# Attention scores of a macaron transformer kernel: one fp32 product replaced by three fp32r products of high and low parts

## The reference, cut to what matters

```
scale = DH ** (-0.5)                                   # H = 16 heads, DH = 64, 512 tokens
q = jnp.einsum('btc,hdc->bhtd', x, Wq)
k = jnp.einsum('btc,hdc->bhtd', x, Wk)
...
v = jnp.einsum('bthe,bted->bhtd', mix_v, proj_v)       # top-2 of 8 experts per head
scores = jnp.einsum('bhid,bhjd->bhij', q * scale, k)
probs = jax.nn.softmax(scores, axis=-1)
attn = jnp.einsum('bhij,bhjd->bihd', probs, v)
...                                                    # top-2 of 8 output experts, Wo
```

## Time and profile before

| | |
|---|---|
| median of three runs | 2796.3 us (2793.99 to 2802.63) |
| the profiled execution's own time | 2803.4 us |
| its span, first to last instruction | 2801.5 us |
| mean granted clock of TensorE | 0.966 of 2.4 GHz |
| PE busy | 2579.3 us, 92% of the span |
| DVE busy | 2187.3 us, 78% |
| ACT busy | 1855.6 us, 66% |
| POOL busy | 737.2 us, 26% |

### The profile page before, as it was taken

How to read it: one execution, slowest core, us unless ns; L and a number is a source line. 1 busy time by engine, 2 the same in 40 slices (tenths; PEclk the granted TensorE clock), 3 DMA queues, 4 the chain that set the end, 5 groups by cost and what they waited for, 6 DMA issues and landing times.

```text
span 2801.5 us, 51283 instructions
## 1 busy us (share of the span) xinstructions
PE 2579.3 (92%) x17437; PEld 1712.1 (61%) x17437; DVE 2187.3 (78%) x3233; ACT 1855.6 (66%) x4430; POOL 737.2 (26%) x564
## 2 busy tenths in 40 slices
PE   4499999998999998999899999999999999899997
PEld 2366665665666655666565665656566665666665
DVE  5688776889889788987987889797777878775552
ACT  2256665867678576875776867687677768666563
POOL 1000000345045214512540443064144315410000
PEclk8699999999999999999999999999999999999998
DMA  3234353564565646546464654666466465545434
GB/s 134 71 114 119 97 145 97 140 174 125 144 155 146 165 112 170 152 125 163 132 171 109 171 146 138 147 167 173 112 176 172 130 159 144 161 124 149 108 80 91
DMA packets 753407, 385.77 MB, mean 138 GB/s; under 512 B 421568, under 2 KB 678656, under 8 KB 752768
## 3 DMA queue, kind: packets, MB, share of 16 engines
q1 hardware_dynamic: 749216, 380.79, 51.4%
q10 hardware_dynamic: 3936, 1.70, 0.2%
HBM read 274.91 MB, written 115.87 MB: 139 GB/s over the span
## 4 chain that ended last, share of the span: by engine, by line
PE 59%; DVE 22%; issue 9%; ACT 3%; DMA 3%; POOL 2%; SPq 1%; DVEq 0%; ACTq 0%; POOLq 0%
PE ps L723 12%; PE ps L732 11%; PE ps L745 11%; PE ps L792 7%; DVE h_ring L1223 6%; PE ps L712 6%; PE ps L798 3%; DVE h_nmax L1043 3%; PE ps L805 2%; DVE h_ring L1233 2%; PE ps L764 1%; POOL h_ring L659 1%; PE ps L832 1%; ACT h_prob L891 1%; DVE h_wide_a L1195 1%
## 5 line engine op out<-in xcount | busy, mean ns | idle before, releaser
L891 ACT ACTIVATE h_prob<-ps,h_nmax 128x512 f32<-128x512 f32 x1024 | 710.6, 696 | 141.6 <-DVE h_nmax L1043 139.6
L1043 DVE TENSOR_REDUCE h_nmax<-ps 128x2 f32<-128x1024 f32 x512 | 621.9, 1215 | 142.7 <-PE ps L723 142.4
L732 PE MATMUL ps<-ident,h_prob 128*128 128x128 f32 x4096 | 623.6, 279 | 27.0 <-DVE h_probT L1283 15.2
L732 PEld LDWEIGHTS ps<-ident,h_prob 128*128 128x128 f32 x4096 | 481.2, 144 | 197.8 <-issue 120.9
L723 PE MATMUL ps<-h_qk 64*128 64x512 f32 x2048 | 587.6, 651 | 0.9 <-ACT h_prob L891 0.8
L668 POOL TENSOR_TENSOR h_wide_c<-h_wide_c,h_ring 128x512 f32<-128x512 f32 x240 | 331.1, 1380 | 731.7 <-DVE h_ring L1233 731.7
L1011 ACT ACTIVATE h_probT<-ps 128x512 f32<-128x512 f32 x796 | 478.7, 601 | 60.8 <-PE ps L732 57.9
L745 PE MATMUL ps<-h_probT,h_v_sb 128*64 128x256 f32 x4096 | 502.7, 388 | 5.8 <-DMA h_v_sb<-v_d 3.6
L745 PEld LDWEIGHTS ps<-h_probT,h_v_sb 128*64 128x64 f32 x4096 | 273.4, 137 | 314.5 <-issue 145.2
L1223 DVE TENSOR_TENSOR_SCAN h_ring<-h_ring 128x512 f32<-128x512 f32 x256 | 397.3, 1552 | 37.6 <-POOL h_ring L659 21.3
L659 POOL TENSOR_TENSOR h_ring<-h_m_xpad,h_m_b_rows 128x512 f32<-128x512 f32 x256 | 349.7, 1376 | 259.0 <-DVE h_m_xpad L1342 250.0
(11 more groups left out here) (222 smaller groups left out, 2678.5 us busy)
## 6 DMA issues: line engine op xcount, KB each, us to landing
h_mix_diag<-mix_blocks SPq DMA_DIRECT2D x128, 512.0 KB, 3.9
v_d<-h_v_mixed SPq DMA_DIRECT2D x128, 256.0 KB, 4.3
h_v_sb<-v_d SPq DMA_DIRECT2D x128, 256.0 KB, 3.4
at_d<-h_att SPq DMA_DIRECT2D x128, 256.0 KB, 2.8
h_mo_diag<-mo_blocks SPq DMA_DIRECT2D x128, 256.0 KB, 3.4
h_att<-at_d SPq DMA_DIRECT2D x128, 256.0 KB, 3.7
h_m_b_rows<-dbl_d SPq DMA_DIRECT2D x128, 256.0 KB, 4.3
h_m_c_rows<-dbl_d SPq DMA_DIRECT2D x128, 256.0 KB, 4.3
```

The lines of the kernel that those rows point to most:

```text
L732: ins = pe.transpose(ps[:, TB + v % 2, k * P:(k + 1) * P], prob[:, v % NB, k * P:(k + 1) * P], ident[:, :])
L891: act.activation(prob[:, v % NB, :], ps[:, SB + v % 4, :], ACT.Exp, bias=nmax[:, p, j, o:o + 1], accum_out=den[:, p, j, o:o + 1]).then_inc ...
L1043: dve.tensor_reduce(nmax[:, p, j, :], ps[:, SB + 2 * w % 4:SB + 2 * w % 4 + 2, :], X, ALU.max, negate=True).then_inc(sem("row_max"), 1)
```

## The change

q and k are now kept as a high part in fp32r (`qk_hi`) and a low part in fp32r (`qk_lo`), and the scores are the sum of three products, as in `three_passes`. ACT reads the PSUM bank twice: once to `qk_hi`, once to the fp32 tile `qk_raw` (one buffer). POOL computes `qk_lo` = `qk_raw` - `qk_hi`. `pq` moves from step 8p-5 to 8p-9 and `pk` from 8p-4 to 8p-5; `drive` moves one step earlier. To make room in SBUF, `x_prep`, `x_post`, `nrm` and `nT` become one tile `x_io`, `g_rest` is written over `gates`, `chosen` holds one gate's choice at a time, and the weights' staging tile at the start lies in `prob` and not in `qk`.

```diff
-            + [(8 * p - 5, "pq", p) for p in range(PAIRS)] + [(8 * p - 4, "pk", p) for p in range(PAIRS)],
+            + [(8 * p - 9, "pq", p) for p in range(PAIRS)] + [(8 * p - 5, "pk", p) for p in range(PAIRS)],
...
-            x_prep = t("x_prep", [P, J, D])
-            x_post = t("x_post", [P, J, D])
-            nT = t("nT", [P, S])
+            x_io = t("x_io", [P, J, D])
+            ln["nrm"] = nrm = x_io
+            nT = x_io[:, :, :].rearrange("p j c -> p (j c)")
...
-            g_rest = t("g_rest", [P, J, H * E])
-            chosen = t("chosen", [P, 2, J, H * E])
+            chosen = t("chosen", [P, J, H * E])
...
-            qk = t("qk", [P, 2, 2, S])
+            qk_hi = t("qk_hi", [P, 2, 2, S], F32R)
+            qk_lo = t("qk_lo", [P, 2, 2, S], F32R)
+            qk_raw = t("qk_raw", [P, S])
...
@@ SyncE, post: the second load of x
-                                if u == 14:
+                                if u == 20:
                                     if n >= 1:
                                         sp.wait_ge(sem("x_out"), 16 * n)
-                                    sp.dma_start(x_post[:, :, :], rows(x_in[n])).then_inc(sem("x_post_in"), 16)
+                                    if n + 2 < NJ:
+                                        wait_full(sp, "gate", 1, n + 2)
+                                        sp.wait_ge(sem("nT_split"), n + 3)
+                                    sp.dma_start(x_io[:, :, :], rows(x_in[n])).then_inc(sem("x_post_in"), 16)
...
@@ SyncE, prep: the first load of x
-                                    if n >= 2:
-                                        sp.wait_ge(sem("normed"), n)
-                                    sp.dma_start(x_prep[:, :, :], rows(x_in[n])).then_inc(sem("x_prep_in"), 16)
+                                    if n >= 3:
+                                        sp.wait_ge(sem("x_out"), 16 * (n - 2))
+                                    else:
+                                        wait_full(sp, "gate", 1, n - 1)
+                                        sp.wait_ge(sem("nT_split"), n)
+                                    sp.dma_start(x_io[:, :, :], rows(x_in[n])).then_inc(sem("x_prep_in"), 16)
...
@@ GpSimd
+                    def low_part(what, p, n):
+
+                        m = 0 if what == "pq" else 1
+                        wait_taken(pool, what, p, n)
+                        pool.tensor_tensor(qk_lo[:, p % 2, m, :], qk_raw[:, :],
+                                           qk_hi[:, p % 2, m, :].bitcast(F32), ALU.subtract).then_inc(sem("qk_lo"), 1)
...
-                                    if u == SCAN_AT[v] - 1:
+                                    if u == SCAN_AT[v] - 2:
                                         drive(n, v)
...
+                            elif kind == "heads":
+                                for p in range(PAIRS):
+                                    for what in ("pq", "pk"):
+                                        if u == AT[what, p] + 2:
+                                            low_part(what, p, n)
...
@@ TensorE, scores
                         if j == 0:
-                            wait_taken(pe, "pk", p, i)
+                            pe.wait_ge(sem("qk_lo"), 2 * (PAIRS * i + p + 1))
                         if w >= 2:
                             pe.wait_ge(sem("prob"), 2 * w - 2)
-                        for o in range(2):
-                            ins = pe.matmul(ps[:, SB + 2 * w % 4 + o, :], qk[o * DH:(o + 1) * DH, p % 2, 0, j * P:(j + 1) * P],
-                                            qk[o * DH:(o + 1) * DH, p % 2, 1, :], start=True, stop=True)
+                        for k_, (q_, k) in enumerate(((qk_hi, qk_hi), (qk_lo, qk_hi), (qk_hi, qk_lo))):
+                            for o in range(2):
+                                ins = pe.matmul(ps[:, SB + 2 * w % 4 + o, :],
+                                                q_[o * DH:(o + 1) * DH, p % 2, 0, j * P:(j + 1) * P],
+                                                k[o * DH:(o + 1) * DH, p % 2, 1, :], start=(k_ == 0), stop=(k_ == 2))
...
@@ ScalarE, take of pq and pk
-                            ins = act.activation(qk[:, c % 2, 0 if what == "pq" else 1, :], bank, ACT.Copy)
+                            act.activation(qk_hi[:, c % 2, 0 if what == "pq" else 1, :], bank, ACT.Copy)
+                            if PAIRS * n + c >= 1 or what == "pk":
+                                act.wait_ge(sem("qk_lo"), 2 * (PAIRS * n + c) + (what == "pk"))
+                            ins = act.activation(qk_raw[:, :], bank, ACT.Copy)
                         elif what == "norm":
-                            if n >= 1:
-                                wait_full(act, "gate", 1, n - 1)
-                                act.wait_ge(sem("nT_split"), n)
-                            ins = act.activation(nT[:, :], bank, ACT.Copy)
+                            ins = act.activation(nT, bank, ACT.Copy)
...
@@ VectorE, top2: chosen is free once the other gate's choice is stored; the rest is written over gates
-                            if a == 1 and i >= 1:
+                            if a == 0 and i >= 1:
                                 dve.wait_ge(sem("mo_out"), 16 * i)
                             link(dve.tensor_copy(pick, key))
...
-                                out=g_rest[:, :, :].rearrange("p j c -> p (j c)"),
+                                out=gates[:, a, :, :].rearrange("p j c -> p (j c)"),
```

More of the change, by code:

```diff
@@ L107, in macaron_kernel @@
         ln = {"stats": sb("stats", [P, J, 6]), "mv": sb("mv", [P, J, 2]), "var_e": sb("var_e", [P, J]),
-              "rstd": sb("rstd", [P, J]), "nrm": sb("nrm", [P, J, D])}
-        nrm = ln["nrm"]
+              "rstd": sb("rstd", [P, J])}
         def links(eng, name):
@@ L278, in macaron_kernel @@
         for kind, n in BASE:
-            for u in range(-8, 110):
+            for u in range(-10, 110):
                 live_at.setdefault(step_of(kind, n, u), []).append((kind, n, u))
@@ L412, in macaron_kernel @@
                 w_load[name] = w.rearrange("h d c -> (h d) c").rearrange("(a p) c -> p a c", p=P)
-            qk_f32 = qk[:, :, :, :].rearrange("p a b s -> p a (b s)").rearrange("p a (n c) -> p a n c", c=P)
+            qk_f32 = prob[:, :, :].rearrange("p (a b) s -> p a (b s)", a=2).rearrange("p a (n c) -> p a n c", c=P)
             att_flat = att[:, :, :, :].rearrange("p a j c -> p (a j c)")
@@ L578, in _ @@
                                         att2_load(n, c)
-                                if u == 14:
+                                if u == 20:
                                     if n >= 1:
                                         sp.wait_ge(sem("x_out"), 16 * n)
-                                    sp.dma_start(x_post[:, :, :], rows(x_in[n])).then_inc(sem("x_post_in"), 16)
+                                    if n + 2 < NJ:
+                                        wait_full(sp, "gate", 1, n + 2)
+                                        sp.wait_ge(sem("nT_split"), n + 3)
+                                    sp.dma_start(x_io[:, :, :], rows(x_in[n])).then_inc(sem("x_post_in"), 16)
                                 if u == AT["out", 0] + 3:
                                     wait_taken(sp, "out", 0, n)
-                                    sp.dma_start(rows(x_res[b] if kind_ == 0 else out[b]), x_post[:, :, :]
+                                    sp.dma_start(rows(x_res[b] if kind_ == 0 else out[b]), x_io[:, :, :]
                                                  ).then_inc(sem("x_out"), 16)
@@ L639, in _ @@
                                     sp.wait_ge(sem("chosen"), 2 * n + 2)
-                                    sp.dma_start(rows(mo_d[n]), chosen[:, 1, :, :]).then_inc(sem("mo_out"), 16)
+                                    sp.dma_start(rows(mo_d[n]), chosen[:, :, :]).then_inc(sem("mo_out"), 16)
                                 for c in range(NCV):
@@ L1081, in take @@
                             dve.wait_ge(sem("x_post_in"), 16 * (n + 1))
-                            x_ = x_post[:, :, :].rearrange("p j c -> p (j c)")
+                            x_ = x_io[:, :, :].rearrange("p j c -> p (j c)")
                             ins = dve.scalar_tensor_tensor(out=x_, in0=bank, scalar=0.5, in1=x_, op0=ALU.mult,
@@ L1094, in top2 @@
                         JH = J * H
-                        g = (gates[:, a] if r == 0 else g_rest)[:, :, :].rearrange("p j (h e) -> p (j h) e", e=E)
+                        g = gates[:, a, :, :].rearrange("p j (h e) -> p (j h) e", e=E)
                         top = g_top[:, :].rearrange("p (n a) -> p n a", a=1).broadcast_to([P, JH, E])
@@ L1098, in top2 @@
                         key = g_key[:, :, :]
-                        pick = chosen[:, a, :, :].rearrange("p j (h e) -> p (j h) e", e=E)
+                        pick = chosen[:, :, :].rearrange("p j (h e) -> p (j h) e", e=E)
                         linked()
@@ L1132, in mix_gates @@
```

(8 more changed lines are left out.)

## The result

The changed kernel took 2834.48 us (median of four, 2833.36 to 2839.47) against 2797.23 us before. The ratio is 1.0135, with an interval of 1.0114 to 1.0155: some 38 us slower. The forecast was 2721 us.

What follows compares the result with a forecast made beforehand. PE was taken as the limit without the scan, DVE with it. Savings of 53 us without and 31 us with the scan, less 10 for contention, gave 74, rounded 75, from 2796.3: 2721 us; range 2663 to 2825 us (0.80).

Steps and rivals of the forecast that it cites:

- What bounds the kernel: Whole schedule: PE is the limit without the scan; with the scan DVE is full and PE is not.
- the stretches: Eight pair periods beside the scan, each granted part of PE's 1.04 us: 0.44 each, 31 us; periods without scan 53 us.
- The halves of the array: PE's scores: fp32r halves work side by side, three slots in 0.80 us, saving 0.26 us a time, 133 us.
- B: Rival on PE's scores: fp32r does not split the array, 220 us more work, 2986 to 3016 us; chance 0.13.
- E: Rival on PE's scores: each slot waits for its weight load, up to 118 us more, 2914 us; chance 0.03.
- ACT's copies and wait, the bank, the shared tiles and their loads: ACT, PSUM and loads: 154 us more copying, bank held 0.6 us longer, later loads; all taken as 0 us.
- POOL's time: POOL: 256 subtractions at 1.38 us add 353 us, from 26% to some 39% of the span.
- DVE against POOL: DVE slowed by POOL: 0.18 us per subtraction, 47 us in all, 25 beside the scan, 10 on the path.
- C: Rival: POOL and DVE in each other's way, 0.77 us per subtraction beside the scan, 108 us, 2851 us; chance 0.07.
- The rule on weight loads that I weighed: PE's scores: a weight load overlaps matmuls in flight only when its row group differs; weighed as the ground for E.

Runs made afterwards that it cites:

- run 1: The changed kernel with each of POOL's 256 subtractions cut to 8 of 512 columns, all waits, copies and matmuls kept; 2764 us, ratio 0.9876.
- run 7: The changed kernel with three fp32r products only for the 52 pairs without a scan, low parts by POOL, the other pairs fp32; 2791 us, ratio 0.9960.
- run 11: Run 1 with the high times high product alone, the other two products of the scores left out; 2702 us, ratio 0.9633.
- run 8: Run 1 with ACT's second copy cut to 8 columns too; 2762 us, ratio 0.9856.
- run 2: The changed kernel with ACT's fp32 copy written where the low part will stand, POOL subtracting in place, so ACT doesn't wait; 2832 us, ratio 1.0110.
- run 14: Run 7 with ACT's fp32 copy going where the low part will stand, so that ACT waits for nobody; 2790 us, ratio 0.9945.
- run 3: The kernel before with the shared tiles and SyncE's changed waits alone, fp32 scores and steps as before; 2802 us, ratio 1.0000.
- run 5: The changed kernel with low parts made by DVE from PSUM, without POOL's subtractions and ACT's second copy; 2922 us, ratio 1.0416.

## Why the prediction was wrong, point by point

- **What bounds the kernel.** Right with the scan, where DVE is full; too simple without it. By the stretches I let 84 us of 133 come out, 63%; without the subtractions (run 1) 38 of 87 did, 44%. By period it was 22 us with the scan, where I had 31, and 22 without it, where I had 53. PE was busy all through the 14 us that I read, but as its work gets shorter it waits more for DVE and ACT (run 7) and its clock falls (run 11). I had no term for either.
- **The halves of the array.** Right in kind (B and E fell: matmuls start in twos, and the second slot's loads start 0.1 us after the scores do, while the first two matmuls run), wrong in size. I took 0.80 us from a full-height group and measured 0.89. What was missing is the 0.09 us at the far end, where the matmuls go back from two halves to full height; it stood in the second 0.53 us of the fp32 scores. That is 46 us of PE.
- **ACT's copies and wait, the bank, the shared tiles and their loads.** Right at zero, as far as tried: runs 8, 2, 14 and 3. Run 8 leaves a short copy of 8 columns, so it prices the copy's length and not its being there.
- **POOL's time.** Near: 1.43 us for each subtraction against 1.38, but `drive` itself went from 1376 to 1576 ns (1409 in run 1, with `drive` as early), which I left out. 416 us more, not 353.
- **DVE against POOL.** This is the step that failed. I took 0.13 us of DVE for each us of POOL, 47 us in all, 25 of them beside the scan and 10 of those on the path. Run 1 against the changed kernel shows 108 us of DVE and 70 of path; beside the scan it is 95 us of DVE and 63 of path. Two errors. I read the price from the scan alone, and the scan's own part came out below it (31 us); the read and all the other operations of DVE, which I left out, took the larger share. And I put 40% of DVE's extra time beside the scan on the path, where 66% came out (63 / 95). A reason for that would be that POOL, which waits for DVE's read, hands DVE's delay back to it; no run separates this from DVE's being full in more of the time than I counted.
- **TensorE's clock.** No term of mine. It was 0.953 to 0.955 in the changed kernel's executions and 0.957 to 0.965 in run 1's. The executions of the kernel before differ with it: those at 0.958 to 0.960 took 2812 us in the middle and those at 0.966 to 0.968 took 2797, so some 2 us for each 0.001 (an estimate from these; the means of the two kernels are 0.954 and 0.960). By that, some 12 of the 70 us came by way of the clock. It is no cause beside the subtractions, since they alone differ between the two kernels; that TensorE's longer waits are what lowered it is my reading and was not tested.
- **The rivals.** The result is C's mechanism. That the time is near its 2851 us is in part luck: C has 53 us of saving and 108 of cost, where 38 and 70 were measured. Cut by period, run 1 and the changed kernel differ by 63 us in the 73 periods with the scan and by 7 in the others: 63 / 146 = 0.43 us for each subtraction beside the scan, above the 0.38 from which C decides. I gave it 0.07, and against it stood only the mean excess of 0.18 us. The row that spoke for it, DVE at 98%, was the one that counted.
- **The sum with what was measured.** 38 us of saving less 70 of cost is 32 us slower, against the forecast's 84 - 10 = 74 faster. Of these 106 us, 60 are the subtractions and 46 PE's saving: 29 for its size (63% of 46) and 17 for how much of it comes out. The 32 are no check of the 38 and 70, which are both differences to run 1; the changed kernel beside its own kernel before was 37 us slower.

## What to carry to other kernels

A second engine that looks idle is not free room if its operations hold up those of the engine that is the limit: price the work by a run with idle copies of it, not by its own busy time, and put them where the real ones will stand (here they stood elsewhere and cost 95 us in place of 70). Where two limits alternate along a schedule, apply a trade between them only in the stretches where the first one binds: the change loses 1.35% applied everywhere and gains 0.4 to 0.55% applied to the 52 pairs without a scan. A busy time that rises with an unchanged count of instructions is the first thing to look for in the profile after.

## What the runs showed of the hardware

- fp32r matmuls of 64 rows on the two halves of the array run side by side, 0.23 us for two of 512 columns at full clock (2.4 GHz), and weight loads hide under them. Going back from the halves to full height costs 0.09 us, for fp32r and for fp32. The first slot of a group is about 0.1 us longer too, but with full-height matmuls just as with the halves (0.32 and 0.33 us). The Trainium skill (TensorEngine Tiling, Key Properties) says that a change of the tiling mode drains TensorE; the 0.09 us on the way back agree with it, and on the way in no extra time shows. The rule on weight loads that I weighed (in the Trainium skill, TensorE: Matmul & The Clock Gate, it stands under The mechanism) does not hold here: the loads of the second slot start at 1404.40 us, in the same rows in which the first two matmuls run from 1404.30 on, and the second slot starts 0.33 us after the first.
- A subtraction on POOL and a two-input operation on DVE hold each other up: with the subtractions back in (run 1 to the changed kernel) the scan's mean goes from 1543 to 1672 ns, the read's from 751 to 813, and POOL's `drive` from 1409 to 1576. A subtraction on DVE with one input in PSUM stayed at 687 ns (run 5). A fill on POOL reads nothing and leaves the scan at 1528 ns, but DVE's one-input operations between SBUF tiles went from 340 to 1081 ns in one group. I had expected fills to be harmless.
